# Later transposes of split maxima and a later tail, one mask matmul per bank, and normalisations divided over three engines, in a two-layer transformer kernel

## What is computed

```python
# layer 0, attention: 16 heads of 16, rotary q and k, causal mask
q = q * cos + _rotate_every_two(q) * sin      # k likewise
scores = jnp.einsum('bhqd,bhkd->bhqk', q, k) * scale + mask
attn = jax.nn.softmax(scores, axis=-1)
out = jnp.einsum('bhqk,bhkd->bhqd', attn, v)  # then @ Wo.T, + x, layernorm
# layer 0, experts: each token goes through the one expert of its largest gate
# layer 1, attention: a local part (window 128) and a latent part, mixed by a gate
gate = jax.nn.sigmoid(local @ gl_w + remote_h @ gr_w)
mixed = gate * local + (1.0 - gate) * remote_h   # then @ out_w, + x, layernorm
# layer 1, feed forward: a router picks an adapter by a sequence's mean
```

## Time and profile before

| | us |
|---|---|
| median of three runs | 1740.39 |
| lowest, highest run | 1736.76, 1743.93 |
| the profiled execution | 1738.24 |
| its span in the trace | 1736.4 |
| PE busy in the span | 1347.3 (78%) |
| DVE busy | 968.2 (56%) |
| ACT busy | 633.2 (36%) |
| POOL busy | 292.6 (17%) |
| mean granted clock of PE | 0.899 of full speed |

### The profile page before, as it was taken

One profiled execution on the slowest core, in us unless ns is written; L12 is line 12 of the kernel. 1 busy time (PEld: TensorE's weight loads), 2 busy tenths in 40 slices (PEclk: granted clock), 3 DMA queues, 4 the chain that ended last, 5 costly groups with the idle time before them and its releaser, 6 DMA issues. The chain is left out here.

```text
span 1736.4 us, 25416 instructions
## 1 busy us (share of the span) xinstructions
PE 1347.3 (78%) x9117; PEld 863.7 (50%) x9117; DVE 968.2 (56%) x2245; ACT 633.2 (36%) x1201; POOL 292.6 (17%) x278
## 2 busy tenths in 40 slices
PE   4578788888888887605999489888888888888753
PEld 2244544454545455405998345555555555554522
DVE  4365555555555566232777355767665766675632
ACT  0033333333333444303554124344444443435332
POOL 2110110011010100052111322213131313111210
PEclk9798999999999999856999589999989999999975
DMA  3441315142513130093221234304040404030000
GB/s 118 113 113 44 92 44 127 49 115 60 130 45 93 31 84 14 2 361 95 72 71 40 76 101 116 99 19 116 20 116 20 116 20 117 20 95 14 2 13 13
DMA packets 70924, 130.45 MB, mean 75 GB/s; under 512 B 7936, under 2 KB 60816, under 8 KB 67344
## 3 DMA queue, kind: packets, MB, share of 16 engines
q1 hardware_dynamic: 67728, 120.42, 25.3%
q0 software_dynamic: 3072, 8.41, 1.8%
HBM read 84.19 MB, written 43.81 MB: 74 GB/s over the span
## 5 line engine op out<-in xcount | busy, mean ns | idle before, releaser
L469 DVE TENSOR_REDUCE first_maxima<-bank 128x1 f32<-128x512 f32 (+3 forms) x352 | 220.8, 638 | 264.5 <-PE bank L305 263.5
L423 ACT ACTIVATE arena<-pair 128x512 f32<-128x512 f32 x320 | 184.8, 599 | 370.7 <-PE pair L330 369.1
L1420 DVE TENSOR_REDUCE second_maxima<-bank 128x2 f32<-128x512 f32 (+1 forms) x224 | 152.7, 685 | 191.8 <-PE bank L1133 190.7
L1288 ACT ACTIVATE second_probs<-pair 128x512 f32<-128x512 f32 (+1 forms) x256 | 137.5, 541 | 280.8 <-PE pair L1157 279.3
L304 PE MATMUL bank<-first_k_stack,first_q_stack 96*128 96x256 bf16 (+3 forms) x512 | 140.9, 309 | 39.5 <-DVE first_maxima L469 24.9
L284 PE MATMUL bank<-first_xT,w_qkv 128*128 128x512 f32 x256 | 133.7, 652 | 9.7 <-DMA first_xT<-in_xT 4.2
L329 PE MATMUL pair<-first_q_stack,first_k_stack 99*128 99x512 bf16 (+3 forms) x512 | 136.2, 305 | 1.6 <-ACT arena L423 1.1
L305 PE MATMUL bank<-constants_bf 128*128 128x128 bf16 x512 | 101.8, 224 | 0.0
L348 PE MATMUL pair<-arena,first_values 128*32 128x512 f32 (+3 forms) x1024 | 99.2, 506 | 1.4 <-ACT arena L423 1.4
L1154 PE MATMUL pair<-second_q_stack,second_k_stack 99*128 99x256 bf16 (+1 forms) x512 | 98.2, 276 | 2.6 <-ACT second_probs L1288 2.6
L536 POOL TENSOR_TENSOR first_halves<-first_halves 128x512 f32<-128x512 f32 x32 | 40.5, 1266 | 346.6 <-DVE first_halves L454 346.6
(11 more groups left out here) (311 smaller groups left out, 2538.1 us busy)
## 6 DMA issues: line engine op xcount, KB each, us to landing
parked<-first_parts SPq DMA_DIRECT2D x32, 384.0 KB, 2.8
first_q_stack<-parked SPq DMA_DIRECT2D x48, 256.0 KB, 4.8
...
```

Source lines behind the costliest of these rows:

```text
L423: act.activation(PT[:, s:s + len(heads), lo:lo + each], ex[n % 3][:, 0:len(heads) * each].rearrange("p (h q) -> p h q", h=len(heads)), ACT ...
L469: dve.tensor_reduce(nm[:, i, qt, heads[0]:heads[0] + len(heads)], mx[n % 2][:, 0:wide].rearrange("p (h k) -> p h k", h=len(heads)), AX.X, ...
L1288: act.activation(PT[:, s:s + len(heads), lo:lo + each], ex[n % 2][:, 0:len(heads) * each].rearrange("p (h q) -> p h q", h=len(heads)), ACT ...
L1420: dve.tensor_reduce(nm[:, i, qt, heads[0]:heads[0] + len(heads)], mx[n % 2][:, :].rearrange("p (h k) -> p h k", h=len(heads)), AX.X, ALU.m ...
```

## The change

Layer 0. In the list, turn, turned and send come 0.14 to 0.15 of a group later. out, add, stats, root and new come about 0.32 later, turn_x and x_in 0.25, logit and log_in 0.34; v and v_in come 1.05 later. The mask is added once per score bank: the heads of a max unit, and the tiles or heads of an exp unit, get their scores first, and one matmul writes all their diagonal blocks. For that the two key tiles of a mixed exp unit change places, so that their diagonal blocks lie side by side. The 1024 mask matmuls become 672.

Layer 1. z is made by ACT (tiles 0 and 1) and by DVE (tiles 2 and 3, straight from mean and rstd) in the step nb, whose first instruction now makes two values. x is made by POOL, in a step new_x of its own at t+2.32. In the second norm ACT makes two tiles and POOL the other two.

```diff
--- before.py
+++ after.py
@@ class Causal
-    AT = {0: 0, 1: 512, 3: 896, 2: 1024}
+    AT = {0: 0, 3: 512, 1: 640, 2: 1024}
...
-    EXP = [([0], [0]), ([0], [1, 3]), ([1], [0]), ([1], [1, 3]), ([0, 1], [2]),
+    EXP = [([0], [0]), ([0], [3, 1]), ([1], [0]), ([1], [3, 1]), ([0, 1], [2]),
...
@@ schedule0
-            at(g0 - 2.5 + 0.1 * i, "v", b, i)
+            at(g0 - 1.45 + 0.1 * i, "v", b, i)
...
-            at(t - 0.90, "turn", b, g)
-            at(t - 0.83, "turned", b, g)
-            at(t - 0.83 + 0.03, "send", b, g)
+            at(t - 0.76, "turn", b, g)
+            at(t - 0.68, "turned", b, g)
+            at(t - 0.68 + 0.03, "send", b, g)
...
-            at(t + 1.18 + 0.14 * i, "out", b, i)
-            at(t + 1.28 + 0.14 * i, "add", b, i)
-        at(t + 1.42, "stats", b)
-        at(t + 1.5, "root", b)
-        at(t + 1.6, "new", b)
+            at(t + 1.5 + 0.12 * i, "out", b, i)
+            at(t + 1.6 + 0.12 * i, "add", b, i)
+        at(t + 1.76, "stats", b)
+        at(t + 1.84, "root", b)
+        at(t + 1.92, "new", b)
...
@@ layer0_attention, PE
                         for x, hh in enumerate(heads):
-                            h, o = i * GH + hh, mx[n % 2][:, x * wide:(x + 1) * wide]
-                            pe.matmul(o, q[0:ROWS, h, qt * P:(qt + 1) * P], k[0:ROWS, h, 0:wide], start=True, stop=True)
-                            ins = pe.matmul(o[:, wide - P:wide], m["idb"][:, :], m["mS0"][:, :], start=False, stop=True,
-                                            skip_group_check=True)
+                            pe.matmul(mx[n % 2][:, x * wide:(x + 1) * wide], q[0:ROWS, i * GH + hh, qt * P:(qt + 1) * P],
+                                      k[0:ROWS, i * GH + hh, 0:wide], start=(x == 0), stop=True, skip_group_check=True)
+                        o = mx[n % 2][:, 0:len(heads) * wide].rearrange("p (h k) -> p h k", k=wide)
+                        ins = pe.matmul(o[:, :, wide - P:wide], m["idb"][:, :], spread(m["mS0"][:, :], P, len(heads)),
+                                        start=False, stop=True, skip_group_check=True)
...
@@ layer1, ACT
                         act.wait_ge(lp["nb"], b + 1)
-                        for t in range(NT):
-                            ins = act.activation(z[:, t, :], x[:, t, :], ACT.Identity, bias=nb[:, 1, t:t + 1], scale=rstd[:, 1, t:t + 1])
+                        for t in range(2):
+                            ins = act.activation(z[:, t, :], x[:, t, :], ACT.Identity, bias=nb[:, t:t + 1], scale=rstd[:, 1, t:t + 1])
                         ins.then_inc(lp["z"], 1)
-                        for t in range(NT):
-                            ins = act.activation(x[:, t, :], x[:, t, :], ACT.Identity, bias=nb[:, 0, t:t + 1], scale=rstd[:, 0, t:t + 1])
-                        ins.then_inc(lp["new"], 1)
@@ layer1, DVE
                         dve.wait_ge(lp["rstd"], b + 1)
-                        for n in range(2):
-                            ins = dve.scalar_tensor_tensor(out=nb[:, n, :], in0=mv[:, :, 0], scalar=-1.0, in1=rstd[:, n, :],
-                                                           op0=ALU.mult, op1=ALU.mult)
-                        ins.then_inc(lp["nb"], 1)
+                        dve.scalar_tensor_tensor(out=nb[:, :], in0=mv[:, 0:2, 0], scalar=-1.0, in1=rstd[:, 1, 0:2],
+                                                 op0=ALU.mult, op1=ALU.mult).then_inc(lp["nb"], 1)
+                        for t in range(2, NT):
+                            ins = dve.tensor_scalar(z[:, t, :], x[:, t, :], mv[:, t, 0:1], rstd[:, 1, t:t + 1], ALU.subtract, ALU.mult)
+                        ins.then_inc(lp["z"], 1)
@@ layer1, POOL
+                    elif kind == "new_x":
+                        pool.wait_ge(lp["z"], 2 * (b + 1))
+                        for t in range(NT):
+                            ins = pool.tensor_scalar(x[:, t, :], x[:, t, :], mv[:, t, 0:1], rstd[:, 0, t:t + 1], ALU.subtract, ALU.mult)
+                        ins.then_inc(lp["new"], 1)
+                    elif kind == "new2":
+                        pool.wait_ge(lp["rstd2"], b + 1)
+                        for t in range(2, NT):
+                            ins = pool.tensor_scalar(x[:, t, :], x[:, t, :], mv[:, t, 0:1], rstd[:, 0, t:t + 1], ALU.subtract, ALU.mult)
+                        ins.then_inc(lp["new2"], 1)
```

42 lines of the change are left out of this document (23 added, 19 removed).

## The result

The changed kernel takes 1698.31 us, the median of four runs (1697.06 to 1700.19), beside 1742.16 for the kernel before on the same chip. The ratio is 0.9736, with a 95% interval of 0.9675 to 0.9797. That is faster, and within the range that was given (1652 to 1717), 15 us above the 1683 forecast. Of all the runs in this document only one, 1715.47 us of e5_tail_back, is more than 1.5% above the fastest of its kernel.

A forecast was written before the change was run, and what follows sets the result against it. The prediction took PE to set the time of both layers. Terms of -44 in layer 0 and -13 in layer 1 gave -57 from 1738.2, so 1681, or 1683 us at the median, with a range of 1652 to 1717.

The forecast's parts named there:

- layer 1: Layer 1: dividing z and x among engines makes z ready earlier and shortens PE's waits, -13 us, ends -25 and +8.
- turn: Layer 0: later transposes of the split maxima no longer wait for DVE's last split, -46 us, bounds 40 and 49.5.
- sends: Layer 0: sends issued later land about 1 us short in the last groups and behind the stack's DMAs, +3 us.
- the clock's -12: Layer 0: half-clock stretches behind the transposes' wait go with it, -12 us of up to 23 lost, ends 0 and 20.
- masks: Layer 0: 352 of 1024 mask matmuls go, about 6 ns each, -2 us, ends 0 and 3.
- tail and v: Layer 0: the later tail puts more on DVE, so PE waits 5 us per batch, not 3: +13, bounds -10 and +35.
- the walk: Both queues followed in layer 0's tail: PE waits 2.6 us for a maxima reduction, 2.4 for new.
- rival B: Layer 0's tail: DVE becomes the bound, PE waits 7 to 8 us per batch, the clock falls behind each; 1715, chance 0.18.
- The last sign: Layer 0: the prediction is wrong if PE's waits there sum to over 80 us.
- rival E: Layer 0: the maxima's rows land too late for exp 0, PE waits 2 us in 32 groups; 1749, chance 0.03.
- rival D: Layer 1: POOL's six new instructions per batch hold up DVE, +8 in place of -13 us; 1704, chance 0.11.
- The last batch: End of layer 1: ACT's 2.07 us halve while POOL does the other two tiles, -1 us, 0 at worst.

The follow-up runs named there:

- e5_tail_back: The changed kernel with v and the tail back where they were before, and turn, turned and send at t-0.515, -0.475, -0.47: 1704.6 us, ratio 0.9781.
- e3_masks: The kernel before with the merged mask matmuls alone: 1741.1 us, ratio 1.0012 to the kernel before.
- e1_turn: The kernel before with turn, turned and send alone moved later, to t-0.515, -0.475 and -0.47: 1713.3 us, ratio 0.9857 to the kernel before.
- e6: The changed kernel with layer 0's stats to log_in later by 0.16 to 0.4 of a group: 1676.6 us, ratio 0.9603 to the kernel before.
- e9: The changed kernel with stats to log_in later in layer 0 and POOL's u_r later in layer 1: 1670.53 us, ratio 0.9577 to the kernel before.
- e10: The kernel of e9 with layer 1's links from rl on later by 0.03 to 0.12 of a group: 1681.8 us, ratio 0.9651 to the kernel before.
- e7: The changed kernel with POOL's u_r in layer 1 moved behind its four instructions for x: 1683.0 us, ratio 0.9646 to the kernel before.
- e2: The kernel before with v and the batch's tail (out to log_in) alone moved later: 1751.4 us, ratio 1.0072 to the kernel before.

## Why the prediction was right, and where it was off

The forecast was -57 on the profiled execution; it came to -39.1, and to -46 by the ratio of all runs. Without the clock the forecast was -32 in layer 0 and -13 in layer 1, -45 in all, and the measured clean change is -44.3. That these agree to 1 us is in part luck: the turn gave more, the sends and v cost more, and 1.6 come from the setup and the routing, where nothing was changed but the place of v. **The step that failed is the clock's -12:** it measured -4.3 in layer 0 (0 to -7 by the other profiles of either order: 36.3, 32.2 and, with the masks merged, 37.0 lost before; 32.0, 30.4 and 30.1 after). The +9.6 of layer 1, for which the prediction had no term, is chance.

| term | forecast | measured | from |
|---|---|---|---|
| turn | -46 | -49.5 | L312's wait gone entirely |
| masks | -2 | -1.2 to -2.7 | e3_masks, clean; start to start |
| tail and v | +13 | +11.0 | tail's waits 24.3 to 17.5, maxima +11.1, banks +6.7 |
| sends | +3 | +7.6 | L328, 0.4 to 8.0 |
| v out of the setup | none | +3.7 | 16 matmuls (3.7 us) moved into the layer; the setup ends 1.0 earlier, but its end lies between 63.9 and 66.3 in thirteen profiles |
| layer 1 | -13 | -13.4 | clean |
| routing and experts | 0 | -0.6 | |
| clock, layer 0 | -12 | -4.3 | 36.3 to 32.0 lost |
| clock, layer 1 | 0 | +9.6 | 56.1 to 65.7 lost; chance |

**The turn** was right in mechanism and place; the 3.3 that I kept back from layer 1 did not come. **The tail**: the walk had PE waiting 2.6 and 2.4, and it waits 2.77 and 1.46. The marker that I set for it was wrong, though: 35 us for the rows of turn_x and the maxima together, where these rows had 37.3 before (24.9 and 12.4) and +13 makes 50. They came to 51.2, near the 55 that was to speak for B, with the forecast's own waits. The last sign was set wrong in the same way: "over 80" for the waits of layer 0, where 129 before and -46, +13 and +3 make 99, and 97 were measured. **The clock**: the argument was that 12 of 14 dips stood behind the turn's wait, so they would go with it. They did, and e1_turn and e5_tail_back put the worth of this at 5 to 15 us where the tail stays. But the tail's new waits bring dips of their own, and longer ones: rival B's second half, "the clock falls behind each", without its first half, the waits of 7 to 8 us. It is also what the prediction's sign for B says (half clock behind the last maxima), and the clock over the earlier trace rows's window went to 0.95, not to 0.98. I had priced that only in the rival, though the forecast itself had waits of 5 us at that place. Had the -12 been taken as nothing for that reason, the forecast would have been 1695. **The sends**: 3 was too little, for one wait of 5.2, behind the stack. The trace before had that send ending its issue at 121.02 and the exp at 127.45 waiting 0.4 for it; it was the row for the largest landing, 6.4 us, and I had taken 3.6 from one send without a stack ahead of it. That also made rival E look further away than it was: e6, e9 and e10 pay 20 to 23 us for it.

**Layer 1** came out at the sum, by terms that were off. z is earlier by 1.6, not 1.2, and L1206 waits 9.8 less, not 8; at 29.4 it is above the 20 of its sign, which the forecast's own -8 did not give either. POOL's tile of x takes 1.22 us, where I had 0.3 to 0.6 from L1539; yet DVE's rows beside it are hardly longer (L1382 at 0.68 in the median and 0.77 at most), so rival D did not come. One cost of that kind is there: the first of DVE's two tiles of z takes 0.79 in seven of eight batches, as it meets POOL's L1542, and 0.40 otherwise; the sum had 0.6 for it. With these rows the rule that I had weighed can be judged. For DVE's L1477, which has two inputs, the trace agrees with the exclusive lock that the Trainium skill describes in "SBUF — State Buffer", section "SBUF: two separate sides": 2.30 beside the 2.33 of POOL's L1551 (two inputs), and in e7 0.58 beside the 0.61 of L1542 (one input). For POOL's tensor_scalar of x it does not: DVE's L1382 has two inputs and takes 0.77 at 1369.01, within the first 1.22 us of POOL's row, where it takes 1.40 beside L1551 (e7). The measurement decides, and the price of D is none. **The last batch** gave nothing back at its end: two tiles on POOL take 2.42, four on ACT took 2.07, where I had -1.

**The other signs.** L313's wait came as said (none). The waits for sends are 8.0, where under 5 was said and 64 would have been E. For the masks the prediction gave 352 instructions to L306 and to L335 alike; L306 has 352 and L335 has 320, together the 672 of the change.

**What stays open.** The clock's loss in layer 1 lies between 49.6 and 66.0 us in thirteen profiles, by chance as far as these runs show: one and the same layer 1 lost 52.0 and 65.7. What makes one execution luckier than another was not found. That dips in layer 0 go with PE's longer waits is shown by their places (357, and e1 and e2), but not every such wait has one: of the 32 of L312 before 12 did, and of e1's five of 2.2 us three.
